# Two-layer graph network on one core: edge matrices applied ahead of the gather, and the first GRU woven into the last attention groups

## What is computed

```python
h = relu(layernorm(x))
# layer 0: attention over the edges, residual product, one GRU cell
Wh = h @ W.T + b_W
e = leaky_relu(s_s[src] + s_d[dst] + a_b[0], 0.2)
attn = softmax of e over the edges that enter dst
a = segment_sum(attn[:, None] * Wh[src], dst) + h @ res_W.T + res_b
x = x + gru(a, h)
# layer 1
h = node_feat = relu(layernorm(x))
for _ in range(4):
    trans = einsum('nd,tod->tno', h, W_edge) + b_edge[:, None, :]
    a = segment_sum(trans[etypes, src], dst, num_segments=N)
    h = gru(a, h)          # r, z: sigmoid; n: tanh(inn + r * hn); (1 - z) * n + z * h
x = x + h
```

## Time and profile before

| | before |
|---|---|
| median of 3 runs | 559.11 us (559.04 to 559.24) |
| the profiled execution | 557.4 us |
| its span, first to last instruction | 555.2 us |
| PE busy | 471.2 us (85%), 3680 matmul instructions |
| DVE busy | 261.5 us (47%) |
| ACT busy | 183.4 us (33%) |
| mean granted PE clock | 0.953 of full |
| chain that ended last | PE 66%, DVE 18%, issue 8%, ACT 4% |

### The profile page before, as it was taken

The page is one execution under the profiler, slowest core; times in us unless marked ns, Lnnn a source line. Parts: engine busy times, 40 slices in busy tenths (PEclk is TensorE's granted clock), DMA queues, the critical chain, the costliest instruction groups (busy, mean ns, idle before and its releaser), DMA issues.

```text
span 555.2 us, 10020 instructions
## 1 busy us (share of the span) xinstructions
PE 471.2 (85%) x3680; PEld 404.7 (73%) x3680; DVE 261.5 (47%) x644; ACT 183.4 (33%) x298; POOL 11.8 (2%) x27
## 2 busy tenths in 40 slices
PE   0479975877777776989699999899989999899995
PEld 0356654666656676969488898788978889788893
DVE  7945889999999982381201223112230222302224
ACT  0421134464876783330511223122221222212221
POOL 5100000000000000001000000000000000000000
PEclk9956999899999997999699999999999999999998
DMA  7000000000000000000000000000000000000001
GB/s 167 1 0 0 1 1 2 0 2 1 1 1 2 2 2 4 1 2 2 4 1 1 2 1 1 0 1 1 2 2 1 1 1 1 1 1 1 0 1 46
DMA packets 5847, 3.65 MB, mean 7 GB/s; under 512 B 500, under 2 KB 5641, under 8 KB 5797
## 3 DMA queue, kind: packets, MB, share of 16 engines
q1 hardware_dynamic: 3188, 1.76, 1.3%
q10 hardware_dynamic: 2608, 1.19, 0.9%
HBM read 2.31 MB, written 0.64 MB: 5 GB/s over the span
## 4 chain that ended last, share of the span: by engine, by line
PE 66%; DVE 18%; issue 8%; ACT 4%; DVEq 3%; DMA 0%; POOL 0%; SPq 0%; ACTq 0%; POOLq 0%
PE big L1280 31%; PE small L1290 6%; PE big L1067 5%; DVE cell_hot L724 5%; PE big L1110 3%; DVE exp_a L763 2%; DVE absent L746 2%; PE small L1166 2%; PE small L1160 2%; PE small L1164 2%; PE small L1162 2%; PE small L1165 2%; PE small L1161 2%; PE small L1102 2%; ACT hn L389 1%
## 5 line engine op out<-in xcount | busy, mean ns | idle before, releaser
L1280 PE MATMUL big<-nibbles,store 128*128 128x256 fp8e4 (+1 forms) x1624 | 179.3, 271 | 6.8 <-issue 3.4
L1280 PEld LDWEIGHTS big<-nibbles,store 128*128 128x128 f16 x1624 | 158.9, 98 | 25.3 <-issue 7.9
L1067 PE MATMUL big<-cell_hot,store 128*128 128x320 bf16 x420 | 72.4, 319 | 26.1 <-DVE cell_hot L724 24.1
L724 DVE TENSOR_SCALAR cell_hot<-iota,cell_w,fields 128x640 bf16<-128x640 f16 x210 | 77.4, 441 | 24.3 <-PEq L1138 8.8
L1067 PEld LDWEIGHTS big<-cell_hot,store 128*128 x420 | 52.2, 144 | 47.0 <-issue 41.0
L561 ACT ACTIVATE store<-big 128x1024 f32<-128x1024 f32 x20 | 20.5, 1023 | 106.3 <-PE big L1280 106.3
L929 DVE SCALAR_TENSOR_TENSOR store<-small,store 128x256 f16<-128x256 f32 x20 | 8.5, 424 | 89.9 <-ACT store L566 89.8
L823 DVE SCALAR_TENSOR_TENSOR store<-store 128x256 f32<-128x256 f32 x25 | 10.6, 425 | 77.1 <-ACT store L503 77.1
L1290 PE MATMUL small<-store,wT 128*128 128x256 f32 x160 | 37.8, 379 | 0.0
L501 ACT ACTIVATE store<-small,gb 128x256 f32<-128x256 f32 x22 | 10.4, 473 | 73.4 <-PE small L1166 73.4
L937 DVE TENSOR_TENSOR store<-small,probT 128x256 f32<-128x256 f32 x20 | 8.5, 424 | 48.6 <-PE small L1290 47.2
(11 more groups left out here) (202 smaller groups left out, 568.4 us busy)
## 6 DMA issues: line engine op xcount, KB each, us to landing
xn<-in_x SPq DMA_DIRECT2D x1, 576.0 KB
out<-wn SPq DMA_DIRECT2D x4, 128.0 KB
store<-in_edge_attr SPq DMA_DIRECT2D x1, 256.0 KB
wn<-in_L_gnn_W_edge ACTq DMA_DIRECT2D x1, 256.0 KB, 7.5
wn<-in_L_gnn_Wi ACTq DMA_DIRECT2D x1, 192.0 KB, 4.7
wn<-in_L_gnn_Wh_g ACTq DMA_DIRECT2D x1, 192.0 KB, 5.0
wn<-in_L_gnn_W_ih ACTq DMA_DIRECT2D x1, 192.0 KB, 7.1
wn<-in_L_gnn_W_hh ACTq DMA_DIRECT2D x1, 192.0 KB, 7.4
```

The source lines that it names most:

```text
L724: last = v.tensor_scalar(cell_hot[:, slot], iota[:], cell_w[:, half, bass.ds(tile + slot, 1)], fields[:, 1, bass.ds(tile + slot, 1)], ALU. ...
L1067: last = mm(big[:, 2 * half + b, 0:HALF], lane_hot[:, :, bass.ds(tile + slot, 1)].rearrange("p l a -> p (l a)"), cell_hot[:, slot, b * HAL ...
L1280: last = mm(big[:, q + t // 2, (t % 2) * CH:(t % 2) * CH + w], h16[parity][:, i, part], A8[:, t % 2, i, c * CH:c * CH + w, t // 2], start= ...
```

## The change

1. **Edge matrices first.** `m16` replaces `h16` and `Bs`: for each source tile, `features` multiplies the features by all four edge matrices at once (one fp32 matmul of 512 columns), `features_in` (DVE) adds the bias row `edge_rows`, `split_hi` (ACT) and `split_lo` (DVE) split the 512 columns in two fp16 halves. `gather` still has 80 matmuls for each chunk, but all of them now add into one PSUM region of 256 columns (`psA` or `psD` in turn), and `messages_in` scales the result by a power of two. `mix`, `b_out`, `split_turn`, `degrees`, `bedge` and the bias product are gone. A scale for the edge matrices (`edge_up`, `edge_down`) is worked out from their norms by ACT, POOL and DVE and applied after the second attention group; the edge matrices' transposes move from the start to there (`edge_weights`, `edge_biases`).
2. **Interleaving.** `first_cells` and the whole-array second norm are gone. After group 9's windows each engine has a list written out by hand, in which the first GRU, the second norm (POOL now takes two tiles at a time, `chunk_scale`), `features` of step 0 and the first 8 source tiles of `gather` for chunks 0 and 1 stand between what is left of attention groups 7, 8 and 9.
3. **Smaller edits.** The branch on `V.general` comes once, behind all this. The four steps are written out, without a loop. The last chunk's gates and cells have 226 columns in place of 256. `cell_gates` writes r and hn first and z last. `attention_in` moves from DVE to ACT. In the last step output chunks are transposed and stored as they come.

```diff
-        h16 = [carve([NT, 2, P], F16, 2) for q in range(2)]
-        Bs = carve([2, TYPES, CH], F32, 4)
+        m16 = [carve([NT, 2, TYPES * P], F16, 2) for q in range(2)]
...
+            def features(s, i):
+                if s == 0:
+                    pe.wait_ge(X.hT, i // 2 + 1)
+                else:
+                    pe.wait_ge(G.h, NCH * s + i // 2 + 1)
+                    pe.wait_ge(T.full, NT * s + i - 1)
+                mm(big[:, i % 2], h1[:, i * P:(i + 1) * P], wT[:, W_EDGE:NWT].rearrange("p t o -> p (t o)"),
+                   start=True, stop=True).then_inc(T.ps, 1)
+            def gather(s, c, tiles):
+                g, w = NCH * (s + 1) + c, width(1, c)
+                if tiles[0] == 0 and g > NCH + 1:
+                    pe.wait_ge(G.aS, g - 1)
+                for i in tiles:
+                    pe.wait_ge(T.lo, NT * s + i + 1)
+                    for part in range(2):
+                        for t in range(TYPES):
+                            last = mm((psA, psD)[g % 2][:, 0:w], m16[s % 2][:, i, part, t * P:(t + 1) * P],
+                                      A8[:, t % 2, i, c * CH:c * CH + w, t // 2],
+                                      start=(i == 0 and part == 0 and t == 0),
+                                      stop=(i == NT - 1 and part == 1 and t == TYPES - 1), skip_group_check=True)
...
+            def features_in(s, i):
+                n = NT * s + i
+                dve.wait_ge(T.ps, n + 1)
+                if n >= 2:
+                    dve.wait_ge(T.lo, n - 1)
+                v.tensor_tensor(full[:, i % 2], big[:, i % 2], edge_rows[:], ALU.add).then_inc(T.full, 1)
+            def split_lo(s, i):
+                dve.wait_ge(T.hi, NT * s + i + 1)
+                v.tensor_tensor(m16[s % 2][:, i, 1], full[:, i % 2], m16[s % 2][:, i, 0],
+                                ALU.subtract).then_inc(T.lo, 1)
...
-            degrees(0, 1)
-            turn(NT)
...
-            aggregate(NT - 2)
-            degrees(1, 2)
...
+            residual(0, 2)
+            pe.wait_ge(K.evac, NW)
+            gates_h(0, 0, 0, 0)
+            count_turn(NT - 1)
+            aggregate(NT - 3)
+            gates_x(0, 0, 0, 0, 0)
+            prob_turn(NT - 2, NT)
+            residual(1, 4)
...
+                gather(s, 2, range(NT))
+                next_features(0, 1)
+                cells_h(2)
+                cells_x(2)
+                next_features(2, 3)
+                out_chunk(0)
+                out_chunk(1)
+                gather(s, 3, range(NT))
```

1041 lines of the change are left out of this document (614 added, 427 removed).

## The result

| | before | after |
|---|---|---|
| median | 559.08 us (556.91 to 559.24, 4 runs) | 526.26 us (524.40 to 528.30, 4 runs) |
| the profiled execution | 557.4 us, span 555.2 | 528.3 us, span 526.4 |
| PE busy | 471.2 us, 3680 instructions | 441.4 us, 3132 |
| mean granted PE clock | 0.953 | 0.973 |

The ratio is 0.9411, with an interval of 0.9381 to 0.9441: 5.9% less, where 6.7% was forecast (521.6 us; the range 511 to 535 holds the time). The four runs lie at two levels, 524.4 and 528.2 us; the profile is of the upper one. The mean granted clock of the last row is not an effect of the change: `e0_changed_again`, the same kernel, has 0.949 at a span of 527.1 us.

A forecast was written before the change was run, and what follows sets the result against it. PE was taken as the bound in stage 3, and waits between engines before it. 198.5 - 0.2 + 76.2 + 2.0 + 234.1 + 7.1 = 517.7 us of span, plus 3.9, gave 521.6 us; range 511 to 535.

The forecast's parts named there:

- the start: From kernel start to the end of group 7's transposes: -0.2 us, between -1.5 and +3.
- stretch up to the branch: From group 7's transposes to the branch: 52.4 us of PE work, 20.4 of waits, 2.0 for half clock.
- the branch's gap: PE standing still at the one remaining branch: 3.4 us, after 3.31 and 3.43 at the two before.
- from there to the last gates: Stage 3 behind the branch: gather, gates, features and output transposes, 234.1 us with no gaps expected.
- around the span: Outside the span: 2.2 us around it and 1.7 from profiled execution to median, 3.9 in all.
- Rival 1: PE's clock stays low through the interleaved stretch before the branch: 531 to 543 us; chance 0.10.
- Rival 2: Lists mesh worse, in the stretch or at steps' ends: +8 to +12, 530 to 534 us; chance 0.13.
- rival 5: Next step's features cannot run before a stage 3 step ends: 21 us for three steps, 543; chance 0.02.
- Rival 3: Better meshing before the branch: only 10 to 12 us of waits, no clock fall, 508 to 512 us; chance 0.11.
- Rival 4: Gather's 80 matmuls adding into one PSUM region cost 271 ns each, not 109: +259 us, slower; chance 0.02.
- marks for right: Gather 109 ns apart, 64 us steps, no PE gap over 0.5 us after the branch, branch wait 3.4 us.
- those for wrong: Gather spacing 115 ns or more, `split_lo` gaps at steps' ends, clock 0.5 beyond 225 us, first window after 48 us.

The follow-up runs named there:

- e0_changed_again: Changed kernel measured once more, word for word, as a control with nothing changed; 528.35 us, ratio 0.9432.
- e1: Changed kernel with the edge matrices prepared one attention group earlier and the bias row's copy and PE's wait for it later; 521.46 us, ratio 0.9316.
- e12: Changed kernel with 3 matmuls of two columns more on PE ahead of the first window; 524.02 us, one run.
- e2: Changed kernel with the second chunk's `attention_in` moved on ACT ahead of group 9's exponentials; 520.67 us, ratio 0.9308.
- e6: Changed kernel with the 128 early gather matmuls of chunks 0 and 1 moved to right behind the branch; 536.23 us, ratio 0.9575.
- e11: Changed kernel with 20 matmuls of two columns more on PE ahead of the first window; 521.73 us, ratio 0.9340.
- e9: Changed kernel with the edits of e1 and e2, and group 9's row maximum ahead of the first cell's front on DVE; 515.68 us, ratio 0.9210.
- e4: Changed kernel with 20 matmuls of 320 columns on zeros ahead of PE's wait for the widened edge matrices; 520.11 us, ratio 0.9300.
- e13: e9 with 20 matmuls of two columns more on PE ahead of the first window; 513.76 us, ratio 0.9173.

## Why the prediction came out 4.7 us low

By its own terms, on the profiled execution:

| term | predicted | measured |
|---|---|---|
| the start (end of group 7's transposes) | 198.3 | 202.17, **+3.9** |
| stretch up to the branch (52.4 + 20.4 + 2.0) | 74.8 | 277.97 - 202.17 = 75.8, +1.0 |
| the branch's gap | 3.4 | 2.73, -0.7 |
| from there to the last gates | 234.1 | 519.36 - 280.70 = 238.7, **+4.6** |
| the end | 7.1 | 526.4 - 519.36 = 7.0, -0.1 |
| span | 517.7 | 526.4, +8.7 |
| around the span; median against the profiled execution | 3.9 | 1.9 - 2.0 = -0.1, -4.0 |
| median | 521.6 | 526.3 |

At the span the forecast is 8.7 us off, not 4.7. The row around the span gave 4.0 back: I added 1.7 us from the profiled execution up to the median, and here the profiled execution is of the upper level and the median lies 2.0 below it. That part is luck; e0's median, 528.35, is 6.8 above the forecast.

**The start** was mis-sized in sign. I counted PE's and ACT's added work and found it hidden, which it is (e1 has it all, and from group 0 to group 2 it takes 34.28 us against 34.11), and put the added waits at 0.5 us. The wait for the widened matrices hangs on a chain of ACT, POOL and DVE passes that begins only after group 1's; it ends 2.78 us late, and the one on ACT 1.34. Each is followed by half clock in the changed kernel's two profiles. Order alone (e1) takes 2.3 us or more of this back; the clock's part up to group 1 is 2.2 us, by e12, where it did not fall there. The clock was in my sum as a property of the last stretch only; it can fall behind every added wait.

**The stretch** is right in its sum by two errors that cancel. The waits are 17.1 us, not 20.4, with the longest where I put it and of the size I gave (5.45 against 6.2; e2 shows its cause, the order on ACT). The half clock costs 2.7 in place of 2.0: 222.05 and 232.26 are where products take twice their time. The work comes to 56.0 us in place of 52.4, with idle times in it that are too short to be listed; e2, with the clock full throughout, gives 55.6. The gain that I counted on here is in the trace: the branch is behind PE at 280.70 against 274.62, 6.1 us later and not at the same time as I had it, but with 10 `features` and 128 gathers (22.6 us) done. e6 shows that the part of this that fills waits is the part that pays.

**The branch** was the other step that failed. I took the two gaps of before for its whole price. From the end of the first gap to the first full gather it takes 13.53 us (294.23 - 280.70) where e11, without second gap and half clock, takes 8.68 (288.60 - 279.92): second gap and half clock are 4.85 us and make the +4.6 of that term. Before, neither place showed a second gap, and nothing in those rows could have told where it would fall; that the clock would drop behind 2.7 us of standing still I could have taken from the falls of the earlier trace rows.

**Everything priced by PE's columns** held: gather 109 ns apart, a feature product 0.86 us, a step 63.93 us against 64, no gap at any step's end, the last chunk at 226 columns. 238.7 - 4.85 leaves 233.8 against the predicted 234.1.

**The rivals.** Rival 1 (the clock low through the stretch) did not come: the clock is at half in two short pieces of the stretch (from 218 to 224 and from 232 to 234 us) and full or nearly so between them. The Trainium skill, "TensorE: Matmul & The Clock Gate", section "A second HAM failure mode: psum-queue depth-cycling", would have given 531 or more; the clock does go to and fro here, but behind waits of 1.3 to 5.5 us and not through the whole. Rival 2 did not come either: the stretch's waits are 17.1 us and not above 20.4, and the window with 70.00 of 70 shows no gap at a step's end; it refutes rival 5 as well. Rival 3 did not come (waits of 17.1, not 10 to 12), though other orders reach 13.6 (e2) and 11.2 (e9). Rival 4 is refuted: each matmul is 272 ns long and they start 109 ns apart in one PSUM region. Of the marks for right, "no PE gap over 0.5 us after the branch" failed, by the 1.79; of those for wrong, a clock of 0.5 beyond 225 us came (at 232 and 285). The late start had no mark: the first window is not late, and the loss lies behind it.

## What to carry to other kernels

A wait that is added to PE costs its length and often half speed behind it: in e2 2.3 to 3.5 us of waits taken away brought 5.1 to 7.9, and with the same wait of 2.8 us in it, the way from group 0 to group 1 took 2.2 us more with two falls of the clock (the changed kernel) than without (e12). Judge an edit by the part of the kernel that it touches, against several profiles that share the rest: start and stretch moved by 2 to 3 us here with nothing changed in them. When work is moved to where an engine has room, look for the chain that makes its operand, and start that chain one group earlier. Count a branch on PE at some 7 us here, not at its first gap, and try whether a few idle instructions ahead of it shift the second one away.

## What the runs showed of the hardware

- Behind the changed kernel's branch PE stood still for 2.6 to 3.0 us and then, in seven of ten profiles, a second time, for 0.8 to 2.2 us. The second gap moved by three matmuls when three were put ahead of the branch, and was absent with twenty (e4, e11, e13). PE started again 1.8 to 2.0 us after the transfer of a 16 KB block of instructions in the first gap and 1.3 to 1.5 us in the second. The two branches of the kernel before and its loop's jump had one gap each (3.31, 3.43 and 1.73), each ended 1.8 us after such a transfer.
- The clock fell behind a wait in one profile and, with the same length at the same place, not in another: at 88 us it was 0.50 in the changed kernel behind a wait of 2.78, and 1.00 in e12 behind one of 2.79 (there it fell at 106 us). At 232 us it fell in the changed kernel behind 1.64 and not in e12, behind the same 1.64. Whether this makes the two levels of the changed kernel's runs, 3.8 us apart, is open: no profile of the lower level was taken. e12, which differs by three matmuls of two columns, has 524.02 us, and its profile has less half clock than the two of the upper level at both places.
- POOL's power of two columns took 1.87 us the first time and 0.69 the four later times, with 1.96 for ten columns before. None of it was waited for.
